# A one-core transformer block: the first norm's gain moved behind the transposes, and six edits of order around it

## The reference, cut to what matters

```python
x = x + attn_block(moe_top2(x))          # parts 1 and 2
x = x + moe_top8(cond_attention(x, mask, cond))   # parts 3 and 4

def attn_block(x):                        # part 2
    qkv = x @ Wqkv + bqkv; q, k, v = split(qkv, 3)
    qp, kp = elu(q) + 1, elu(k) + 1
    kv = einsum('bsd,bse->bde', kp, v)                       # key tiles summed per batch
    attn = einsum('bsd,bde->bse', qp, kv) / (qp @ kp.sum(1) + 1e-6)   # output tiles
    x = layer_norm(x + attn, g1, b1)                         # the first norm
    ffn = (silu(x @ Wg + bg) * (x @ Wu + bu)) @ Wd + bd      # feed-forward, hidden width 682
    return layer_norm(x + ffn, g2, b2)

def moe_top8(x):                          # part 4, 16 routed experts and a shared one
    scores = sigmoid(l2norm(x) @ l2norm(gate_w).T)
    w, idx = top_k(scores, 8); w = w / w.sum(-1)
    return sum_e combine[e] * (silu(x @ w_gate[e]) * (x @ w_up[e])) @ w_down[e] + shared(x)
```

## Time and profile before

| | |
|---|---|
| median of three runs | 903.85 us |
| profiled execution, device time | 901.43 us |
| its span | 899.7 us |
| TensorE clock granted, mean | 0.961 |
| PE busy | 819.5 us (91%) |
| VectorE busy | 691.6 us (77%) |
| POOL busy | 406.2 us (45%) |
| ScalarE busy | 363.2 us (40%) |

### The profile page before, as it was taken

How to read it: one execution, slowest core, us unless ns; L and a number is a source line. 1 busy time by engine, 2 the same in 40 slices (tenths; PEclk the granted TensorE clock), 3 DMA queues, 4 the chain that set the end, 5 groups by cost and what they waited for, 6 DMA issues and landing times. The chain is left out here.

```text
span 899.7 us, 17121 instructions
## 1 busy us (share of the span) xinstructions
PE 819.5 (91%) x5386; PEld 734.2 (82%) x5386; DVE 691.6 (77%) x1399; ACT 363.2 (40%) x722; POOL 406.2 (45%) x482
## 2 busy tenths in 40 slices
PE   7699999999995589678999989888999999999997
PEld 4699999999995477567888979756888888888887
DVE  4888888988884588885779779777777777776776
ACT  5466656666551565343332545772111111111110
POOL 4276778777784300125775627402323233232332
PEclk9799999999998699777999999999999999999999
DMA  8436412314512700007000020010010010010002
GB/s 289 123 106 200 140 47 84 92 43 133 199 47 57 228 1 1 1 0 223 2 1 1 1 71 2 1 36 1 19 35 17 17 35 17 17 35 17 17 0 94
DMA packets 45912, 55.20 MB, mean 61 GB/s; under 512 B 5166, under 2 KB 34920, under 8 KB 45864
## 3 DMA queue, kind: packets, MB, share of 16 engines
q1 hardware_dynamic: 41384, 43.59, 15.4%
q0 software_dynamic: 4032, 11.02, 4.0%
q10 hardware_dynamic: 448, 0.01, 0.0%
HBM read 47.00 MB, written 7.60 MB: 61 GB/s over the span
## 5 line engine op out<-in xcount | busy, mean ns | idle before, releaser
L2120 POOL TENSOR_TENSOR kTh<-at_acc,kTh 128x512 fp32r<-128x512 f32 x68 | 88.2, 1297 | 231.5 <-DVE kTh L2235 231.5
L1911 PE MATMUL psum<-act_hi,ff_w 128*128 128x512 f32 x544 | 179.7, 391 | 0.4 <-ACT at_acc L2076 0.4
L2076 ACT ACTIVATE at_acc<-psum 128x512 f32<-128x512 f32 x68 | 40.7, 600 | 237.0 <-PE psum L1911 237.0
L1911 PEld LDWEIGHTS psum<-act_hi,ff_w 128*128 128x128 f32 x544 | 102.3, 188 | 21.0 <-ACT at_acc L2076 0.8
L1952 PEld LDWEIGHTS psum<-ff_w,kTh 128*128 128x128 f32 x816 | 106.6, 191 | 8.9 <-DVE y L2316 3.2
L2316 DVE SCALAR_TENSOR_TENSOR y<-psum,ff_rawd,y 128x256 f32<-128x256 f32 x272 | 112.2, 475 | 0.2 <-PE psum L1952 0.2
L1952 PE MATMUL psum<-ff_w,kTh 128*128 128x256 f32 x816 | 108.7, 283 | 3.1 <-DVE y L2316 3.1
L1911 PE MATMUL psum<-act_lo,ff_w 128*128 128x512 f32 x272 | 106.6, 392 | 0.0
L470 ACT ACTIVATE e_u<-psum,e_bias 128x256 f32<-128x256 f32 x152 | 63.9, 472 | 93.8 <-PE psum L375 93.8
L2232 DVE TENSOR_TENSOR at_acc<-psum,at_acc 128x512 f32<-128x512 f32 x68 | 47.0, 692 | 70.7 <-PE psum L1911 58.2
L774 PE MATMUL psum<-act_hi,ff_w 128*128 128x512 f32 x192 | 63.4, 405 | 4.0 <-DVE ff_h32sb L1527 2.3
(11 more groups left out here) (444 smaller groups left out, 2340.9 us busy)
## 6 DMA issues: line engine op xcount, KB each, us to landing
e_raw<-in_W SPq DMA_DIRECT2D x16, 512.0 KB, 6.7
e_raw<-in_W SPq DMA_DIRECT2D x8, 1024.0 KB, 6.0
v_tok<-in_xT SPq DMA_DIRECT2D x4, 512.0 KB, 9.8
y<-in_x SPq DMA_DIRECT2D x4, 512.0 KB, 10.5
y<-y_rows SPq DMA_DIRECT2D x4, 512.0 KB, 7.3
v_tok<-y_rows SPq DMA_DIRECT2D x4, 512.0 KB, 8.1
v_tok<-in_x SPq DMA_DIRECT2D x4, 512.0 KB, 8.3
e_raw<-in_w_gate SPq DMA_DIRECT2D x16, 128.0 KB, 2.1
```

The lines of the kernel that those rows point to most:

```text
L1911: last = pe.matmul(bank[:, :], e2_w[par][a][:, o + k * H2:o + (k + 1) * H2], actT[b][:, k, g * GT:(g + 1) * GT], start=n == 0, stop=n == 3 ...
L2076: act.activation(sl_sb[:, s % 2, :], ps[s % 2][:, :], ACT.Silu).then_inc(esil, 1)
L2120: pool.tensor_tensor(hh[1][:, s % HS, :], h32[:, s % 2, :], hh[0][:, s % HS, :], ALU.subtract).then_inc(hsp, 1)
```

## The change

It has seven parts.

1. First norm's factors in turned layout. `g1` and `b1` are also loaded as columns (`cols`, two transfers at the stage's start, 128 partitions x 2 numbers each, from addresses 512 bytes apart). The scaled tiles are transposed without gain and bias. Then ScalarE makes the high part from the PSUM bank with gain and bias as per-partition factors, and a second array `less` (high part minus bias), and VectorE makes the low part from bank, gain and `less`. In token layout POOL still applies gain and bias to `y`, now after the transpose, tile by tile, for the residual.
2. Key tiles ahead of outputs. On PE the outputs 6 and 7 come after the last two key tiles. On VectorE the key tiles 14 and 15 are prepared before the outputs that stood ahead of them.
3. Four feed-forward steps stand between outputs in the first stage where there were two, and the vector parts of three of them (`EARLY`, `EARLY_HIDDEN`).
4. Groups 2 and 3 are normed and turned in the feed-forward stage (`TURNED`), between its steps.
5. `Wd` is loaded in the first stage and split in three pieces. The second stage's three broadcast rows are its first transfers.
6. A root activation is issued ahead of the sums (`early`), other PSUM banks are used at the stage's end, and some buffers have new homes.
7. Expert weights by halves. The combine weights of tiles 0 to 7 are made before the first expert's loop, those of tiles 8 to 15 after its fourth step.

```diff
+        EARLY, EARLY_HIDDEN, TURNED = 4, 3, 2
+        def gained_high(act, turn, bank, k, sl, cols, less, firm):
+            act.wait_ge(turned, turn)
+            act.activation(act_hi[:, k, sl], bank, ACT.Identity, scale=cols[:, 0, k:k + 1], bias=cols[:, 1, k:k + 1]).then_inc(firm, 1)
+            act.wait_ge(firm, turn - FIRST_TURN)
+            act.activation(less[:, k, :], act_hi[:, k, sl], ACT.Identity, bias=cols[:, 2, k:k + 1]).then_inc(hi_done, 1)
+        def gained_low(dve, turn, bank, k, sl, cols, less):
+            dve.wait_ge(hi_done, turn)
+            dve.scalar_tensor_tensor(out=act_lo[:, k, sl], in0=bank, scalar=cols[:, 0, k:k + 1], in1=less[:, k, :],
+                                     op0=ALU.mult, op1=ALU.subtract).then_inc(lo_done, 1)
...
                     sp.dma_start(bq[:, :], d["bq_cols"]).then_inc(bq_in, 16)
+                    for n, name in enumerate(("g1", "be1")):
+                        sp.dma_start(cols[:, n, :], d[name].rearrange("(k p) -> p k", p=P), allow_slow_non_contiguous=True).then_inc(cols_in, 16)
...
-                    for i in range(NB, NT):
+                    for i in range(NB - 2, NB + 1):
                         output(i)
-                        if i % TG == TG - 1:
-                            turn("r", i // TG - OL)
+                    turn("r", 0)
+                    output(NB + 1)
+                    output(NB + 2)
                     pe.wait_ge(ff_split, 2)
                     pe.wait_ge(vlo, NT)
-                    for g in range(OL, G):
-                        pe.wait_ge(lo_done, n0 + NQ + KC)
-                        ff_up(pe, ff_w, g - OL, ff_hps)
-                        turn("r", g)
+                    pe.wait_ge(lo_done, n0 + NQ + KC)
+                    ff_up(pe, ff_w, 0, ff_hps)
+                    output(NB + 3)
+                    output(NB + 4)
+                    turn("r", 1)
+                    output(NB + 5)
+                    pe.wait_ge(nuse, NB + 2)
+                    ff_up(pe, ff_w, 1, ff_hps)
+                    output(NB + 6)
+                    output(NB + 7)
+                    for s in range(2, EARLY):
+                        pe.wait_ge(ff_h32d, s - 1)
+                        ff_up(pe, ff_w, s, ff_hps)
...
-                    for g in range(OL):
-                        sl = slice(g * TG, (g + 1) * TG)
-                        pool.wait_ge(scaled, g + 1)
-                        pool.tensor_tensor(y[:, sl, :], y[:, sl, :], group_rows(gb[:, 0, :]), ALU.mult).then_inc(gained, 1)
+                    for g in range(TURNED):
+                        pool.wait_ge(turned, n0 + NQ + (g + 1) * KC)
+                        for i in range(g * TG, (g + 1) * TG):
+                            last = pool.tensor_tensor(y[:, i, :], y[:, i, :], gb[:, 0, :], ALU.mult)
+                        last.then_inc(gained, 1)
                         pool.wait_ge(gained, g + 1)
-                        pool.tensor_tensor(y[:, sl, :], y[:, sl, :], group_rows(gb[:, 1, :]), ALU.add).then_inc(normed[0], 1)
+                        for i in range(g * TG, (g + 1) * TG):
+                            pool.tensor_tensor(y[:, i, :], y[:, i, :], gb[:, 1, :], ALU.add)
+                    for s in range(EARLY_HIDDEN):
+                        pool.wait_ge(ff_hhi, s + 1)
+                        pool.tensor_tensor(hidden_home[1][:, s, :], h32[:, s % 2, :], hidden_home[0][:, s, :], ALU.subtract).then_inc(ff_hsp, 1)
...
+                    dve.wait_ge(cols_in, 32)
+                    ch.link(dve.tensor_scalar(cols[:, 2, :], cols[:, 1, :], -1.0, None, ALU.mult))
                     dve.wait_ge(la_rin, 48)
                     ch.link(dve.tensor_scalar(bkv[:, 0:D], bkv[:, 0:D], 1.0, None, ALU.add))
                     combine(0)
...
+                    output(3)
+                    output(4)
+                    norm(0)
                     finish(1)
...
+                        if s == 3:
+                            for f in range(TURNED, G):
+                                fl = slice(f * TG, (f + 1) * TG)
+                                act.wait_ge(rreq1, f + 1)
+                                act.activation(rstd1[:, fl], rstd1[:, fl], ACT.Sqrt).then_inc(root1, 1)
+                        if s in (4, 7):
+                            norm_group(act, y, TURNED + (s > 4), rstd1, shift1, shifted1, scaled1)
+                        if s in (6, 8):
+                            f = TURNED + (s > 6)
+                            for k in range(KC):
+                                gained_high(act, n0 - (G - f) * KC + k + 1, ps[6 + k % 2], k, slice(f * GT, (f + 1) * GT), cols1, less1, firm1)
...
+                        if s in WIDENED:
+                            r = WIDENED[s]
+                            pool.wait_ge(turned, n0 - (L1 - r) * KC)
+                            for i in range(r * TG, (r + 1) * TG):
+                                last = pool.tensor_tensor(y[:, i, :], y[:, i, :], rows1[:, 0, :], ALU.mult)
+                            last.then_inc(wide, 1)
```

More of the change, by code:

```diff
@@ L818, in stage_linear_attention @@
             kvout, kvps, kvdone, nps, nuse = sem("la_kvout"), sem("la_kvps"), sem("la_kvdone"), sem("la_nps"), sem("la_nuse")
[L819 to L820 removed]
+            densum, gained, cols_in = (sem(f"la_{x}") for x in ("densum", "gained", "colsin"))
+            mv, rstd, shift, cols, rreq, root, shifted, scaled, firm = norm1
             n0 = turns_done[0]
@@ L1056, in _, with first_norm @@
                             halves(half_up(i))
+                    act.activation(early[:, :], ident[:, 0:1], ACT.Sqrt)
                     sums_out(1)
-                    for g in range(G):
+                    def first_norm(g):
                         act.wait_ge(rreq, g + 1)
@@ L2282, in _ @@
                     ch.link(dve.tensor_scalar(lg[:, :, :], lg[:, :, :], 1.0, None, ALU.add))
-                    ch.link(dve.reciprocal(sc[:, :, :], lg[:, :, :]))
-                    hidden(0, 0, False)
-                    for i in range(NT):
-                        last = dve.max(top[:, i, :], sc[:, i, :])
-                    ch.link(last)
-                    hidden(1, 1, False)
-                    for i in range(NT):
-                        last = dve.match_replace(out=rep[:, i, :], in_to_replace=top[:, i, :],
-                                                 in_values=sc[:, i, :], imm_value=-1.0)
```

280 lines of the change are left out of this document (179 added, 101 removed).

## The result

| | before | changed | changed, second set |
|---|---|---|---|
| median | 903.0 us (6 runs) | 897.36 us (6 runs, 896.11 to 900.66) | 896.14 us (6 runs) |
| ratio to before, 95% interval | | 0.9945 (0.9931 to 0.9960) | 0.9923 (0.9904 to 0.9941) |
| profiled execution's span | 899.7 us | 898.7 us | 893.9 us |

The forecast was 891 us with a range of 882 to 899: the time lies in the range and on the forecast's side, but the gain is 5.6 us (7.2 in the second set), where 12.9 were forecast. The second set, of the same kernel, is experiment e5. The first profiled execution was the slowest of its six, and the two profiles of the same code differ by 4.8 us; so the stages are read from several profiles.

What follows compares the result with a forecast made beforehand. PE was taken as the bound, busy 819.5 of 899.7 us, waiting for order on other engines. Terms -2.6 + 10.0 + 2.2 + 3.1 = 12.7 gave 888.7 profiled, plus 2.4 to the median: 891 us, range 882 to 899.

Steps and rivals of the forecast that it cites:

- A: Linear attention's start: VectorE's wait for two column transfers delays combine(0), 2.6 us lost, with nothing absorbing it.
- B: Linear attention's end: earlier key tile 15, norms and transposes, with four feed-forward steps between outputs, gain 10.0 us.
- the walk: Method for changed stages: each engine's entries in new order, starting when predecessor and awaited work are done, durations from rows.
- C: Feed-forward stage: two fewer steps, against added transposes and waits at steps 11 to 13, gain 2.2 us.
- The prediction's own sign: Feed-forward: the forecast is wrong if PE's waits there exceed 6 us.
- The mechanism of ScalarE's order: Feed-forward: ScalarE's gained operations, table loads and root after down(0) make PE wait 1.3, 0.8 and 1.8 us.
- D: Experts' head: weights by halves remove the 2.73 us wait and slow matmuls, one 0.95 us wait remains; 3.1 us gained.
- The forecast that the clock falls between the stages: Between linear attention and feed-forward: PE's idle time before the barrier drops its clock again, costing 2.2 us.
- the first rival: No clock fall between the stages, or fewer feed-forward stalls: feed-forward gains 4.7 to 6 us, time 887 to 889; chance 0.25.
- POOL at 1.24 us a tile: Linear attention's end: slower POOL tile operations end the stage 4 to 7 us later, time 895 to 898; chance 0.15.
- slow columns: Linear attention's start: column transfers take as long as g_bb, 5.8 us more, time 897; chance 0.12.
- all the added work on PE: Feed-forward: without slack, all 23 us of added work stand on PE in place of 2.9, time 911; chance 0.04.

Runs made afterwards that it cites:

- e5: The changed kernel again, unedited, with a second profile; ratio to the kernel before 0.9923, median 896.14 us.
- e6: Changed kernel with outputs 3, 4 and 5 and the first group's statistics again ahead of key tile 15 on VectorE; ratio to before 0.9950.
- e2: Changed kernel with VectorE's wait for the two column transfers moved behind the first combine and first two low parts; ratio to before 0.9906.
- e3: Changed kernel with the combine weights of all 16 tiles made before the first expert's loop, as before the change; ratio to before 0.9954.
- e1: Changed kernel with the two mask transfers issued right behind the three broadcast rows in the feed-forward stage; ratio to before 0.9876.
- e7: Changed kernel with group 3's transposes inside down(0), its high parts ahead of step 8's gate, low parts behind group 0's additions; ratio to before 0.9895.
- e4: Changed kernel with three edits: mask transfers early, column wait late, group 3's transposes inside down(0) with its high and low parts moved; ratio to before 0.9832.
- e8: The kernel of e4 with VectorE's mask counts 1 to 3 moved between the additions of down(0); ratio to before 0.9846.
- e10: The kernel of e4 with three POOL operations (bias for groups 1 and 2, gain for group 3) moved earlier, counts unmoved; ratio to before 0.9838.
- e9: The kernel of e8 with three POOL operations (bias for groups 1 and 2, gain for group 3) moved earlier; ratio to before 0.9828.
- e11: Changed kernel with only three POOL operations (bias for groups 1 and 2, gain for group 3) moved earlier; ratio to before 0.9911.

## Why the prediction was off

- **A, the start: 2.6 us forecast, 3.2 found** where it arises. The transfers landed in 2.1 and 2.4 us, not 1.7. The text held that nothing absorbs it. By the profiles with and without the wait, 0.5 us of it is left on average at the stage's end. Half is gone by the first key tile, with PE at half clock in either case; that the rest goes in clock falls, which differ from execution to execution, is likely and not shown.
- **B, the end: the path right, the sum partly by luck.** A and B together were to give 7.4 us; the profiles show 7.0, 7.3 and, in variants with the same linear attention, up to 8.2. But with the wait late, where A is gone, the five profiles gain 8.0 us on average and not the 10.0 of B. So A cost about 2 us less and B gave about 2 us less than forecast. B's lack is there at key tile 15 already: done at 72.4 to 73.6 us in those five, where the walk without A has 70.2 (367.1 less 296.9). Clock falls between 14 and 43 us into the stage, which the profile before does not show, are likely part of it; the cause stays open. POOL's last low part set the end as forecast, its tile operations took 0.70 us and not 1.24, and e6 shows the keys' share.
- **C, feed-forward: the step that failed.** Forecast 2.2 us gained, found 2.8 (second profile) to 6.7 us (first) lost. The prediction's own sign came: PE's waits in this stage were to stay under 6 us, and those over 0.3 us sum to 9.8 us in the first profile and 8.8 in the second (before: 2.7). Of the second profile: up to `down(0)` 8.1 us were gained and not 6.0, for the clock did not fall at the stage's start. From there to step 8's first matmul it took 13.85 us where 9.6 were forecast (8.70 as before and 0.9 for the transposes). The walk had no wait of PE inside `down(0)`: it put that term at nothing, without a reason. The runs show one of 1.9 to 3.3 us in all five profiles of this code (e2, e3, e5, e6 and the first), for additions that stand on VectorE behind a mask count, which itself stood 1.7 to 3.6 us for its transfer, and in three of the five (the first, e2, e5) a clock fall with it. With the mask early alone (e1) the stretch takes 13.01 us, with group 3 moved alone (e7) 13.65, with both 9.51, 9.58 and 9.51 (e4, e8, e10), the forecast's figure, and 11.29 in e9, where VectorE was 1 us late at the count as in e1. So the late mask is what the walk lacked, since it left SP's list out of this stage; that VectorE's own list is late enough for a wait of 1.5 to 1.7 us in some executions is the other part. From step 8 to `down(1)` 3.85 us were lost where 2.9 were forecast: the waits stood at steps 11, 12 and 13 as forecast, 1.20, 0.53 and 2.47 us in place of 1.3, 0.8 and 1.8. The mechanism of ScalarE's order was right, and e7 shows it, but 1.0 of the 2.47 us is POOL's (e11). In `down(2)` 1.8 us were lost behind a small VectorE operation that lasted longer while POOL worked, which the walk allowed for in linear attention alone; e11 takes it away. (The text read the fourth idle time of this stage before as 0.16 us; the trace has 0.75, at 479.56. It is there in both kernels and moves the sum by little.)
- **D, the head: 3.1 forecast, 2.6 found**, with the one wait of 0.95 us forecast and 0.98 found; e3 agrees.
- Summed for the second profile: linear attention 7.3, feed-forward -2.8, experts 2.6, less 1.2 us by which the untouched first part was longer: 5.8 with the roundings, and the spans differ by 899.7 - 893.9 = 5.8. Of the 6.9 us that lack to the 12.7 forecast, 5.0 are C's, 1.2 the untouched part's, 0.5 D's and 0.1 A's and B's.
- **Rivals.** The forecast that the clock falls between the stages was wrong for both profiles of the changed kernel, and the first rival right on that, but its price was lost elsewhere. In the variants it fell there in e4 and e10 and, a little later, in e6, behind the same idle time of 2.3 us, so one profile could not tell. POOL at 1.24 us a tile, slow columns, and all the added work on PE did not come.

## What to carry to other kernels

When a stage is made shorter from the front, list every transfer issued in it with its landing time and the first instruction that wants it: what had landed 1.4 us early now stands at the head of an engine's queue, and everything behind it pays. Put work that one engine does in a burst (here four gained operations and two table loads) into the gap that the timeline shows beside another engine's long step (`down(0)`, where ScalarE stood still for 15.9 us). Before a step of the forecast is called right, look whether its parts are right too: here two errors of 2 us in one stage cancelled. And profile more than one execution before a stage is explained to the microsecond.

## What was not expected of the hardware

- The same idle time of TensorE brings its clock down in one execution and not in another: behind 3.06 us it went to 0.50, behind 3.26 us (e3, same code there) it stayed at 1.00; behind 2.47 us it went to 0.50 in the first profile and in e1 and stayed in the second, e2, e3 and e6. Between the five profiles of the same feed-forward code the stage differs by up to 5 us (115.96 to 120.98), nearly as much as the whole change brings.
- After the long stand at linear attention's start, the full clock came back at times that differ between executions of the same code: 6.6 to 9.6 us behind PE's first transposes in seven profiles that start late (7.4 in the first, 6.6 in the second, 9.6 in e7), and 6.6 to 9.9 us in the five that start 3.2 us earlier (9.9 in e2 and e4, 6.6 in e8, where it fell again at 14 us).
- VectorE's operation on 8 columns took 1.58 us while POOL ran an operation of 1.30 us, and 0.21 us (before) and 0.23 us (e11) without it.
